# Stack loads of queries and keys issued a fixed plan time ahead of their first pass

## The reference, cut to what matters

```python
def mha(x, mask, Wi, bi, Wo, bo):
    qkv = x @ Wi.T + bi
    q, k, v = jnp.split(qkv, 3, axis=-1)          # then [B, H=16, T=1024, 8]
    scores = jnp.einsum('bhqd,bhkd->bhqk', q, k) / math.sqrt(8) + mask   # causal + ALiBi
    attn = jax.nn.softmax(scores, axis=-1)
    out = jnp.einsum('bhqk,bhkd->bhqd', attn, v)
    return out.transpose(0, 2, 1, 3).reshape(B, T, D) @ Wo.T + bo

for i in range(4):
    x = x + mha(layer_norm(x, ln1_w[i], ln1_b[i]), mask, ...)
    h = gelu(layer_norm(x, ln2_w[i], ln2_b[i]) @ ffn1_w[i].T + ffn1_b[i])
    x = x + (h @ ffn2_w[i].T + ffn2_b[i])
```

## Time and profile before

| what | value |
|---|---|
| times of the kernel | 3360.95, 3368.85, 3370.55 us (median 3368.85) |
| the profiled execution | 3376.56 us, of which the span 3374.8 us |
| busy in the span | PE 2632.2 us (78%), PEld 1113.1 (33%), DVE 1938.5 (57%), ACT 1426.5 (42%), POOL 580.1 (17%) |
| granted TensorE clock, mean | 0.841 |
| DMA | 129.88 MB, 64,218 packets, share of the 16 engines 10.7% |
| the decoder's attention | first pass of task 0 at 89.9 us, last second pass at 1605.7 us |
| issues of the stack's rows of maxima | 192 DMAs of 4 KB, 1.6 / 2.2 / 16.2 us to landing (min / median / max) |

### The profile page before, as it was taken

One profiled execution on the slowest core, in us unless ns is written; L12 is line 12 of the kernel. 1 busy time (PEld: TensorE's weight loads), 2 busy tenths in 40 slices (PEclk: granted clock), 3 DMA queues, 4 the chain that ended last, 5 costly groups with the idle time before them and its releaser, 6 DMA issues. The chain is left out here.

```text
span 3374.8 us, 38611 instructions
## 1 busy us (share of the span) xinstructions
PE 2632.2 (78%) x12745; PEld 1113.1 (33%) x12745; DVE 1938.5 (57%) x4374; ACT 1426.5 (42%) x2500; POOL 580.1 (17%) x595
## 2 busy tenths in 40 slices
PE   6489898979979798998676898862566695888847
PEld 4233333333424233332232344330222342222225
DVE  2376666656757565774255723348999524766243
ACT  2155555545646554666243032333333242355510
POOL 1100111110101111100055001004878201000000
PEclk7599988988979897999678998875888797798978
DMA  2211212120211212110100000000000002110010
GB/s 69 87 64 42 81 39 77 48 87 30 77 55 68 73 39 77 38 57 24 40 1 6 1 0 23 0 13 0 0 0 0 25 0 87 40 38 31 14 76 13
DMA packets 64218, 129.88 MB, mean 38 GB/s; under 512 B 18698, under 2 KB 34442, under 8 KB 60334
## 3 DMA queue, kind: packets, MB, share of 16 engines
q1 hardware_dynamic: 64020, 127.42, 10.7%
HBM read 92.30 MB, written 34.08 MB: 37 GB/s over the span
## 5 line engine op out<-in xcount | busy, mean ns | idle before, releaser
L1432 ACT ACTIVATE sb_prob<-ps 128x512 f32<-128x512 f32 (+1 forms) x1216 | 651.8, 575 | 545.3 <-PE ps L1243 407.0
L1243 PE MATMUL ps<-sb_q_stack_half,sb_k_stack_half 81*128 81x512 bf16 (+2 forms) x1792 | 482.9, 326 | 150.8 <-DMA sb_q_stack_half<-sb_max_rows 100.0
L1217 PE MATMUL ps<-sb_k_stack_half,sb_q_stack_half 78*128 78x512 bf16 (+3 forms) x1536 | 493.2, 356 | 42.2 <-DMA sb_q_stack_half<-alibi 26.6
L1353 DVE TENSOR_REDUCE sb_row_max<-ps 128x1 f32<-128x512 f32 x512 | 347.3, 687 | 239.9 <-PE ps L1217 238.1
L1362 DVE CUSTOM_DVE_ANT_0 sb_masked_scores<-ps,sb_mask_row 128x128 bf16<-128x128 f32 (+3 forms) x512 | 228.6, 488 | 184.5 <-PE ps L1217 183.9
L1362 DVE CUSTOM_DVE_ANT_0 sb_masked_scores<-ps,sb_mask_row,sb_row_max 128x128 bf16<-128x128 f32 (+3 forms) x512 | 274.2, 545 | 105.0 <-PE ps L1217 101.6
L1243 PEld LDWEIGHTS ps<-sb_q_stack_half,sb_k_stack_half 81*128 81x128 bf16 x1792 | 166.2, 101 | 441.2 <-ACT sb_prob L1432 149.6
L1264 PE MATMUL ps<-sb_prob,sb_v_first_half 128*9 128x512 f32 (+3 forms) x2048 | 256.1, 575 | 0.0
L624 DVE CUSTOM_DVE_ANT_0 sb_masked_scores<-ps,sb_mask_row 128x128 f32<-128x128 f32 (+7 forms) x256 | 183.5, 756 | 107.7 <-PE ps L553 106.5
L2557 POOL TENSOR_TENSOR sb_inflow<-sb_delta_u,sb_b_spread 128x1024 f32<-128x1024 f32 x64 | 233.2, 3668 | 45.9 <-ACT sb_b_spread L2540 45.9
L1217 PEld LDWEIGHTS ps<-sb_k_stack_half,sb_q_stack_half 78*128 78x128 bf16 x1536 | 154.4, 105 | 216.9 <-DVE sb_row_max L1362 54.7
(11 more groups left out here) (407 smaller groups left out, 4266.8 us busy)
## 6 DMA issues: line engine op xcount, KB each, us to landing
sb_q_stack_half<-q_rows SPq DMA_DIRECT2D x192, 96.0 KB
sb_k_stack_half<-k_rows SPq DMA_DIRECT2D x96, 192.0 KB
o_rows<-sb_o_raw SPq DMA_DIRECT2D x64, 256.0 KB, 6.6
sb_k_stack_half<-k_rows SPq DMA_DIRECT2D x96, 96.0 KB
q_rows<-sb_qk_parts SPq DMA_DIRECT2D x48, 128.0 KB, 2.1
k_rows<-sb_qk_parts SPq DMA_DIRECT2D x48, 128.0 KB, 2.2
sb_k_stack<-k_parts SPq DMA_DIRECT2D x24, 192.0 KB
sb_q_stack<-q_parts SPq DMA_DIRECT2D x8, 576.0 KB
```

Source lines behind the costliest of these rows:

```text
L1217: pe.matmul(M.ps[:, k % RING, 0:hi - lo], qst[half][0:S1_ROWS, s, j, at:at + P], kst[half][0:S1_ROWS, s, lo // CH, j, 0:hi - lo], start=Tr ...
L1243: mm = pe.matmul(bank[:, x * w + lo:x * w + hi], kst[half][0:S2_ROWS, s, t // 4, j, t % 4 * P:(t % 4 + 1) * P], qst[half][0:S2_ROWS, s, j, ...
L1353: dve.reduce_max(rowmax[:, tau % 3, 0, at:at + 1], M.ps[:, k % RING, 0:w], AX_X).then_inc(first_done, 1)
L1432: act.activation(prob[:, st % PROB_STEPS, heads[0]:heads[-1] + 1, a:CH], scores.rearrange("p (j q) -> p j q", j=len(heads)), ACT.Exp).then ...
```

## The change

One constant and one function are new, and one line moves the duty of each stack to a later step:

```diff
+STACK_AHEAD = 16.0
 ...
+        def earlier(s, us):
+            s0 = s
+            while s and self.steps[s0]["end"] - self.steps[s - 1]["end"] < us:
+                s -= 1
+            return s
 ...
             latest[(half, self.slot[tau])] = tau
+            s = max(s, earlier(first_step[self.task_first[tau]], STACK_AHEAD))
             duty.setdefault(s, []).append((4, "stack", tau))
```

## The result

The changed kernel takes 3261.7 us in the median of 4 runs (3259.5 to 3270.0), against 3364.9 for the kernel before in 4 runs on the same chip. The ratio is 0.9702, with a 95% interval of 0.9669 to 0.9736. The forecast was 3258, in a range of 3230 to 3312. The profiled execution took 3259.5 us, with a span of 3257.7 (before: 3376.6 and 3374.8).

The account below looks back on a forecast made before the run. PE was taken to set the pace in the decoder, busy 1276 of 1455 us. Removed 136.4 less added 25.9 gave 110.5 us net, 3376.6 to 3266, then 7.7 less for plain runs: 3258, range 3230 to 3312.

Parts of the forecast that it names:

- The five waits: PE's second pass at tasks 20, 28, 36, 44, 52 waits for rows of maxima; all go, 72.1 us.
- task 0's: PE's second pass of task 0 waits for its rows behind stacks 4 to 6; goes, 27.0 us.
- The clock: PE's lower clock level behind the five waits comes back, 30 us (bounds 0 and 30).
- Task 1 and task 13: New PE waits: task 1's rows 4.5 us plus 3 for lower clock; task 13's stack 4.4 us.
- The reciprocal: DVE's reciprocal waits behind stack 29's load and its like, stopping PE too; six places, 14 us added.
- The projection's wait: PE's wait at 370.30 for normalised heads behind stacks 16 to 18; goes, 6.4 us.
- The unmoved stacks: First-pass waits of tasks 0, 7, 15, 23 to 63, which don't move, stay at 26.6 us.
- The spare times: Moved loads land before PE's first pass: stack 29 tightest with 4.6 us, others 6 to 12; price 0.
- My point on the late loads: Rival E: first pass waits for its stack at every moved task, eating the gain or slower, 3474; chance 0.05.
- The sum: Removed 136.4 less added 25.9, net 110.5 us off the profiled 3376.6, giving 3266, or 3258 for plain runs.

Follow-up runs that it names:

- fifteen loads alone: Kernel before, with only the first three stacks of half 0 in each round from task 24 on moved later; 3275.2 us, ratio 0.9741.
- Wide loads: Kernel before, duties unmoved, loads of k and q walked feature by feature so the outermost extent is 8 instead of 3; 3238.7 us, ratio 0.9634.
- behind heads: Changed kernel with the stacks of tasks 21, 29, ..., 61 put behind duty heads instead of ahead; 3251.2 us, ratio 0.9639 to the kernel before.
- The run with 8 us: Changed kernel with a plan time ahead of 8 instead of 16 us; 3433.1 us, ratio 1.0204 to the kernel before.
- wide loads and 12 or 16 us ahead: Changed kernel plus loads of outermost extent 8, plan time ahead 12 or 16 us; 3187.9 us (ratio 0.9447) at 12, 3190.1 us (0.9453) at 16.
- wide loads and 8 us ahead: Changed kernel plus loads of outermost extent 8, plan time ahead 8 instead of 16 us; 3266.4 us, ratio 0.9689 to the kernel before.

## Why the prediction was right, step by step

- **The five waits and task 0's.** Right in place, cause and size. The rows land 3.0 us after their issue at tasks 20, 28, 44 and 52, some 5 us ahead of PE, as the sum had it (3.8 us at task 36). The run with fifteen loads alone shows that the five places and their clock are worth 86 to 101 us. Wide loads show that the cause had two parts, as the sum had them.
- **The clock.** 27 us were forecast net, and PE's busy time fell by 32. Some of the nearness is luck. With fifteen loads alone PE's busy time in the attention fell by 40 us (1303.1 to 1262.7), where I had 30, and the other 39 moves gave 9 back (1271.4), where I had 3 for task 1 and nothing behind the reciprocal's waits. The two errors go against each other. These are single executions, and the clock of one kernel's executions differs by up to 0.01, so the 9 us are rough.
- **Task 1 and task 13.** The sum had waits of 4.5 and 4.4 us, and 3 more of clock behind the first. The waits became 2.1 (147.34 us on PE) and 3.2. Stack 4 was issued when reckoned (132.2), but the rows landed at 147.3 instead of 148.5 and PE came at 145.2 instead of 144.0. SP got to stack 13 some 1 us sooner, measured against PE.
- **The reciprocal.** Six waits of 2.0 to 3.0 us, 14 in all, were forecast. Six of 1.3 to 2.3 came, 10.5 in all, and PE's waits for DVE's maxima rose by 11.2 us (13.0 to 24.2). So DVE's wait does pass on to PE nearly whole. That these waits cost time in sum is not shown (behind heads).
- **The projection's wait** of 6.4 us went. **The unmoved stacks** kept theirs but for the 0.9 us of task 47; the entry rose from 26.6 to 31.7 us, mostly by task 13.
- **The spare times** are the step that was off, though it cost nothing. I called stack 29 the tightest, with 4.6 us, and gave the rest 6 to 12. (My point on the late loads then spoke of three with 5 to 6 us, which does not go with that.) By count of issues and landings stack 29 had 9.0, and the tightest were stacks 14, 22, 30, 38, 46, 54 and 62, with 0.8 to 1.9 us. That late loads would not eat the gain was right, but with less room than I gave it. I had read their distance to the first pass from stretches at a low clock. With the clock back PE reaches the same piece sooner: the second pass of task 28 and the first pass of task 30 lie 19.4 us apart before and 11.3 after. A little more speed on PE, or a little less time ahead, turns them into waits. The run with 8 us shows what follows.
- **The sum.** 110.5 us were forecast from the profiled execution, and 117 came. By medians on one chip it was 103. That 3258 is so near to 3261.7 is in part luck: I started from a median of 3368.85, and the kernel before came out at 3364.9 in the comparison.

## What to carry to other kernels

A load that is issued as soon as its slot is free stands in the same queue as the small DMA that someone waits for. Look in the list of waits for a small DMA with a long landing, and ask what was issued just in front of it. Issue each load late enough to stay behind what is urgent, and early enough to cover its own landing at the speed PE will have after the fix; and first make the load itself short, by an outermost dimension that is wide enough. (Here that needs the same order of rows on both stacks.) The best version here is both: wide loads and 12 or 16 us ahead, 5.5% faster than before.

## What the runs showed of the hardware that I had not expected

A load whose DMAs have an outermost extent of 3 held up just three sixteenths of each small DMA behind it: 9 of 48 landings came at 11.8 to 12.2 us and the other 39 within 3.0, and the 9 were enough to stop PE for 14.45 us.

Short waits cost as much again by the clock here. In the kernel with wide loads and 8 us ahead, 18 waits of at most 5.3 us (41.9 us in sum, with 36 us more idle time than at 16 us ahead) came with 45 us of longer busy time, at a granted clock of 0.91 instead of 0.95. And the order of the rows inside one DMA, with the same bytes and the same number of DMAs, changed the landing of a load of half 1 from 15.2 to 9.4 us (task 7).
